# A two-layer attention and expert kernel on one core: the second layer's probabilities turned by VectorE and by transfers in place of TensorE

## The reference

```python
x = x + L0_attention(layernorm(x), ctx)      # 16 heads of width 8
x = x + L0_experts(layernorm(x))             # 8 experts, the best 2 of each row
# second layer, attention: 16 heads of width 64
q, (k, v) = layernorm(x) @ Wq, split(ctx @ Wkv)
dots = q @ k.T * 64 ** -0.5
dots = dots - (1.0 - mask)[:, None, :, None] * 1e6   # mask of the query rows
attn = softmax(dots, axis=-1)
x = x + (attn @ v, heads side by side) @ Wout + bout
x = x + relu(layernorm(x) @ w1 + b1) @ w2 + b2       # width 512
```

## Time and profile before

| | |
|---|---|
| time, three runs | 920.72, 922.16, 922.33 us; median 922.16 |
| the profiled execution: span | 938.3 us (no time of its own is given beside it; it is 16.1 us, 1.75%, above the median) |
| TensorE busy | 875.5 us, 93% |
| ScalarE busy | 691.2 us, 74% |
| VectorE busy | 648.8 us, 69% |
| GpSimd busy | 451.7 us, 48% |
| moved by DMA | 104.82 MB, mean 112 GB/s |

### The profile page before, as it was taken

One profiled execution on the slowest core, in us unless ns is written; L12 is line 12 of the kernel. 1 busy time (PEld: TensorE's weight loads), 2 busy tenths in 40 slices (PEclk: granted clock), 3 DMA queues, 4 the chain that ended last, 5 costly groups with the idle time before them and its releaser, 6 DMA issues.

```text
span 938.3 us, 28898 instructions
## 1 busy us (share of the span) xinstructions
PE 875.5 (93%) x8397; PEld 783.1 (83%) x8397; DVE 648.8 (69%) x2020; ACT 691.2 (74%) x2694; POOL 451.7 (48%) x765
## 2 busy tenths in 40 slices
PE   5889999999999859999997899999999999999996
PEld 3667777777767759999997799999999999999995
DVE  6787888888787652222224888887778777777873
ACT  3988898989889822333336999998877887887782
POOL 3134454544435361111115777776666666666542
PEclk9999999999999988999999999999999999999998
DMA  6896676766767412222231122222211221222110
GB/s 167 247 235 215 199 225 205 217 217 214 238 216 227 121 62 68 68 67 67 73 101 29 40 65 63 62 68 66 65 60 43 67 61 41 65 64 62 36 52 9
DMA packets 114371, 104.82 MB, mean 112 GB/s; under 512 B 10932, under 2 KB 101430, under 8 KB 114294
## 3 DMA queue, kind: packets, MB, share of 16 engines
q1 hardware_dynamic: 107394, 89.64, 31.9%
q0 software_dynamic: 6112, 13.90, 4.8%
q10 hardware_dynamic: 788, 0.39, 0.1%
HBM read 57.32 MB, written 46.58 MB: 111 GB/s over the span
## 4 chain that ended last, share of the span: by engine, by line
PE 82%; issue 5%; DVE 4%; ACT 3%; DMA 2%; SPq 2%; POOL 2%; another core or an unknown queue 0%; POOLq 0%; DVEq 0%
PE bank L1388 10%; PE bank L1155 8%; PE bank L1201 8%; PE bank L1403 7%; PE bank L1360 7%; PE bank L1367 7%; PE bank L1413 6%; PE bank L1474 6%; PE bank L1462 4%; PE bank L1193 4%; PE bank L1485 3%; PE bank L1312 3%; PE bank L1272 2%; PE bank L1177 2%; ACT PR L680 2%
## 5 line engine op out<-in xcount | busy, mean ns | idle before, releaser
L680 ACT ACTIVATE PR<-PR,nmx 128x128 f32<-128x128 f32 x512 | 198.1, 391 | 3.8 <-DVE nmx L881 0.4
L680 ACT ACTIVATE PR<-bank,nmx 128x128 f32<-128x128 f32 x512 | 187.0, 427 | 1.1 <-DVE nmx L881 1.1
L345 POOL TENSOR_TENSOR PR<-PR,rden 128x512 f32<-128x512 f32 x128 | 133.4, 1042 | 98.5 <-DVE rden L886 92.3
L1155 PE MATMUL bank<-ident,PR 128*128 128x128 f32 x1024 | 154.9, 276 | 3.1 <-POOL PR L345 1.0
L1155 PEld LDWEIGHTS bank<-ident,PR 128*128 128x128 f32 x1024 | 120.0, 142 | 43.9 <-issue 38.8
L680 ACT ACTIVATION_READ_ACCUMULATOR PR<-bank,nmx 128x1 f32 x512 | 137.1, 268 | 0.0
L774 ACT ACTIVATE H<-bank 128x512 f32<-128x512 f32 x70 | 41.8, 597 | 91.9 <-PE bank L1360 91.9
L1388 PE MATMUL bank<-XCT,wqk 128*128 128x128 f32 x832 | 103.6, 278 | 0.7 <-ACT XCT L668 0.7
L1388 PEld LDWEIGHTS bank<-XCT,wqk 128*128 128x128 f32 x832 | 96.9, 192 | 3.5 <-ACT XCT L668 1.0
L680 ACT ACTIVATION_READ_ACCUMULATOR PR<-PR,nmx 128x1 f32 x512 | 97.1, 190 | 0.0
L881 DVE TENSOR_REDUCE nmx<-bank 128x4 f32<-128x512 f32 x128 | 86.0, 673 | 7.3 <-PE bank L1193 7.1
(11 more groups left out here) (182 smaller groups left out, 2017.9 us busy)
## 6 DMA issues: line engine op xcount, KB each, us to landing
second_layer_values<-wide SPq DMA_DIRECT2D x32, 512.0 KB
wide<-second_layer_values SPq DMA_DIRECT2D x32, 512.0 KB
expert_outputs<-HF SPq DMA_DIRECT2D x32, 256.0 KB
expert_outputs<-HF SPq DMA_DIRECT2D x64, 128.0 KB
KBD<-expert_outputs SPq DMA_DIRECT2D x64, 128.0 KB
QS<-expert_outputs SPq DMA_DIRECT2D x32, 256.0 KB
PR<-expert_inputs SPq DMA_DIRECT2D x36, 128.0 KB, 2.0
expert_outputs<-PR POOLq DMA_DIRECT2D x35, 128.0 KB, 2.0
```

The costliest lines, as they stand in the source:

```text
L345: nc.gpsimd.tensor_tensor(unit, unit, rden[:, p, G * g:G * g + G].unsqueeze(2).broadcast_to([P, G, P]), ALU.mult).then_inc(s["nm"], 1)
L680: last = nc.scalar.activation(PR[:, g, j * P:(j + 1) * P], scored, ACT.Exp, bias=nmx[:, p, h:h + 1], accum_out=den[:, p, h:h + 1])
L1155: last = nc.tensor.transpose(T_BANK[g % 2][:, j * P:(j + 1) * P], PR[:, g, j * P:(j + 1) * P], ident[:])
```

## The change

The second layer no longer turns the probabilities on TensorE. Instead VectorE turns each unit in blocks of 32 by 32 from `PR` to a new buffer `BT` (`turn_unit`), one instruction a unit, and the blocks are put in their places through DRAM: SP stores half of a sequence (two units, 512 KB) from `BT` to `turned_blocks` (`store_blocks`) and loads it back to `PTC` in four transfers of 128 KB, one for each 32 partitions, in runs of 1 KB (`load_turned`). `transpose_unit` and `read_PT` stay for the first layer alone. Banks 2 and 3 are free by this, and the four units of scores lie in four banks (`S1_BANK`), so that both pairs are multiplied one after the other. ScalarE, not VectorE, copies Y's group 3 (semaphore `yq`). `values` reads `PTC` in runs of 32 elements. TensorE projects group 1 before group 0. All five engines get new orders in `step1`: on ScalarE four `fill_rows` and then all 16 exponentials; on VectorE four row maxima, then the rest; on GpSimd the scaling of unit 2 a step earlier. A few semaphores are merged, with the same meaning. Nothing of what is computed changes.

The core of the diff (the merged semaphores, the lines that adapt the counts in waits, and allocations are left out):

```diff
-        PTC = w1[:, 0:NU, :]
+        PTC = w1[:, 0:NU, :].rearrange("p (a u) c -> p a (u c)", a=2).rearrange("p a (i h b) -> p a i h b", i=4, b=32)
...
+        BT = sb("BT", [P, 2, 2 * G * P])
...
+            def store_blocks(m, half):
+                wait_apart(sp, (c["bt"], NU * m + 2 * half + 2), (c[f"pt{half}"], 64 * m))
+                sp.dma_start(bt_dram[half], BT[:, half, :]).then_inc(c[f"bw{half}"], 16)
+            def load_turned(m, half):
+                wait_apart(sp, (c[f"bw{half}"], 16 * (m + 1)), (c["pv"], NU * (m - 1) + 2 * half + 2))
+                for j in range(4):
+                    sp.dma_start(PTC[32 * j:32 * j + 32, half, :, :, :].rearrange("a i h b -> a i (h b)"),
+                                 bt_dram[half].rearrange("(i a) (j c) -> j a i c", a=32, j=4)[j]).then_inc(c[f"pt{half}"], 16)
             def step1(n, p):
                 q = 1 - p
+                if exists(n - 1):
+                    load_turned(n - 1, 0)
+                    store_blocks(n - 1, 1)
                 if exists(n + 2) and not early(n + 2):
                     load_ctx(sp, c, n + 2, p)
                 if exists(n):
                     wait(sp, c["pv"], NU * (n - 1))
                     sp.dma_start(V1[:, p, :, :].rearrange("p h d -> p (h d)"), v_dram[n]).then_inc(c[f"v{p}"], 16)
+                if exists(n - 1):
+                    load_turned(n - 1, 1)
                 if exists(n - 3):
                     wait(sp, d["x"], n - 2)
                     sp.dma_start(out[n - 3], acc[:, q, :]).then_inc(out_stored[q], 16)
+                if exists(n):
+                    store_blocks(n, 0)
             over_steps(sp, step1, -3, NB + 2, 3, KEYS_AHEAD)
             sp.wait_ge(out_stored[0], 8 * NB)
             sp.wait_ge(out_stored[1], 8 * NB)
@@ -625,7 +646,7 @@
             def step1(n, p):
                 q = 1 - p
                 if exists(n - 1):
...
-                if exists(n - 1):
-                    scale_pool(pool, c, n - 1, q, 3)
-                if exists(n - 2):
-                    norm_pool(pool, d, n - 2, p)
                 if exists(n + 2):
                     norm_pool(pool, c, n + 2, p)
-                if exists(n):
-                    scale_pool(pool, c, n, p, 0)
-                    scale_pool(pool, c, n, p, 1)
                 if exists(n + 1):
                     wait_apart(pool, (c["xn"], n + 2))
                     xrow = X[:, bass.ds(n + 1, 1), :].rearrange("p o d -> p (o d)")
                     nc.gpsimd.tensor_tensor(xrow, xrow, out_bias[:, 0, :], ALU.add).then_inc(c["bias"], 1)
+                if exists(n):
+                    scale_pool(pool, c, n, p, 0)
+                if exists(n - 2):
+                    norm_pool(pool, d, n - 2, p)
+                if exists(n):
+                    scale_pool(pool, c, n, p, 1)
+                    scale_pool(pool, c, n, p, 2)
             over_steps(pool, step1, -3, NB + 2, 3, KEYS_AHEAD)
 
 
...
-                    exponentials(c, n, p, 1)
-                    fill_rows(n, 2)
-                if exists(n - 1):
-                    read_PT(c, n - 1, 3)
-                if exists(n):
-                    fill_rows(n, 3)
-                    exponentials(c, n, p, 2)
-                if exists(n - 1):
-                    read_heads(n - 1, q, 0)
-                if exists(n + 2):
-                    read_xct(c, n + 2, p, not early(n + 2), c["y"], NU * (n + 1))
-                if exists(n - 1):
-                    read_heads(n - 1, q, 1)
-                if exists(n):
-                    exponentials(c, n, p, 3)
+                    act.wait_ge(c["y"], NU * n + NU)
+                    wait(act, c["s"], NU * (n - 1))
+                    nc.scalar.activation(YT[:, p, 3 * G:4 * G, :].rearrange("p h s -> p (h s)"), Y_BANK[3][:],
+                                         ACT.Copy).then_inc(c["yq"], 1)
                 if exists(n + 1):
-                    fill_rows(n + 1, 0)
-                    fill_rows(n + 1, 1)
-                if exists(n):
-                    read_PT(c, n, 1)
-                if exists(n + 1):
-                    exponentials(c, n + 1, q, 0)
+                    read_xct(c, n + 1, q, not early(n + 1), c["y"], NU * n)
+                if exists(n - 2):
+                    read_heads(n - 2, p, 0)
+                    read_heads(n - 2, p, 1)
+                if exists(n):
+                    for g in range(NU):
+                        fill_rows(n, g)
+                    for g in range(NU):
+                        exponentials(c, n, p, g)
             over_steps(act, step1, -3, NB + 2, 3, KEYS_AHEAD)
 
 
...
+                def turn_unit(m, g):
+                    dve.wait_ge(c["nm"], NU * m + g + 1)
+                    wait(dve, c[f"bw{g // 2}"], 16 * m)
+                    nc.vector.transpose(BT[:, g // 2, :].rearrange("p (j h b) -> p h j b", j=4, b=32)[:, G * (g % 2):G * (g % 2) + G],
+                                        PR[:, g, :].rearrange("p (h j b) -> p h j b", h=G, j=4)).then_inc(c["bt"], 1)
 
...
                     keys = key_slot(m) if early(m) else KT1[:, p, :, :]
-                    if isinstance(m, int) and m == 0:
-                        pe.wait_ge(kg["kc"], 2 * KEYS_AHEAD)
-                    wait(pe, c["yc"], NU * m + NU)
-                    wait(pe, c["sh"], NU * m + 2 * pair)
+                    wait(pe, c["sh"], NU * (m - 1) + 2 * pair + 2)
                     for j in range(G):
                         chunk = G * pair + j
                         for r in range(2):
                             half = slice(DH1 * r, DH1 * r + DH1)
-                            last = mm(S_BANK[r][:, j * P:(j + 1) * P], QT1[half, p, chunk, :], keys[half, chunk, :],
+                            last = mm(S1_BANK[2 * pair + r][:, j * P:(j + 1) * P], QT1[half, p, chunk, :], keys[half, chunk, :],
                                       start=True, stop=True)
                             if j == G - 1:
                                 last.then_inc(c["s"], 1)
@@ -1410,22 +1423,20 @@
                     for j in range(G):
                         for r in range(2):
                             half = slice(DH1 * r, DH1 * r + DH1)
-                            last = mm(bank[5 + pair][half, j * P:(j + 1) * P], V1[:, p, 2 * (G * pair + j) + r, :],
-                                      PTC[:, 2 * pair + r, j * P:(j + 1) * P], start=True, stop=True)
+                            last = mm(bank[5 + pair][half, j * P:(j + 1) * P].rearrange("p (i b) -> p i b", i=4),
+                                      V1[:, p, 2 * (G * pair + j) + r, :], PTC[:, pair, :, G * r + j, :], start=True, stop=True)
                             if j == G - 1:
...
+                    if is_sequence(0, n):
+                        pe.wait_ge(kg["kc"], 2 * KEYS_AHEAD)
+                    wait(pe, c["yc"], upto(n, 3, 2))
+                    wait(pe, c["yq"], upto(n))
                     scores(n, p, 0)
+                    scores(n, p, 1)
                 if exists(n - 3):
                     wait(pe, d["xct"], n - 2)
```

134 lines of the change are left out of this document (59 added, 75 removed).

## The result

| | before | after | ratio, 95% interval |
|---|---|---|---|
| time, median of four runs each | 921.44 us | 937.09 us | 1.0186 [1.0162, 1.0211] |
| lowest and highest | 919.52, 922.33 | 935.17, 940.22 | |

The account below looks back on a forecast made before the run. TensorE bounds the kernel before; after the change a loop over three engines was to bind. Start +3.5, early +5.5, late -10 and end +3.4 gave +2.4 on the span, 922.2 + 2.3 = 924.5 us; range 907 to 942.

Parts of the forecast that it names:

- the likeliest case: Three-engine loop in the second layer, with the norm meeting GpSimd's scaling: 924.5 us, own range 917.5 to 931.5, chance 0.38.
- TensorE's clock: Rival: TensorE idles 2.5 us in early steps and its clock falls in a third of them: +11, 935 us; chance 0.11.
- Early steps: Steps with keys made ahead: 12.4 us between first scores, 0.7 longer each, +5.5 us over eight.
- The loop: Second-layer steps run from scores through ScalarE, VectorE and GpSimd back to TensorE: 13.2 us late, 12.4 early.
- Step 4: VectorE turns unit 0 from 7.2 to 7.8; its norm waits for GpSimd's scaling until 8.9; two norms end at 9.4.
- Step 6: Early: reciprocal, turn of unit 1, copy to `XDT` that bank 7 waits for, 10.4; inputs and values: next scores at 12.4.
- The turn: VectorE's block turn of one unit, taken at 0.60 us, like the maximum of 512 columns; four a step.
- The second rival: A VectorE turn takes twice, 1.2 us, and VectorE becomes the bound: 949 us; chance 0.15.
- The first three intervals: Start of the second layer, between first scores: from 10 us growing to 12.4, 33.5 in all, +3.5.
- The way through DRAM: Store 2.9 and load 3.4 us, covered by 3 us: nothing in steps. Rival, late transfers: 940 us, chance 0.11.
- Values in runs of 32 elements: TensorE's values read in runs of 32: taken at nothing, at worst twice the 1.73 us.
- TensorE alone binds: Rival: TensorE's own work sets the second layer, all else hidden: 877 us; chance 0.05.

Follow-up runs that it names:

- e6: Changed kernel with plain transfers in place of the second layer's gathers (routing of the experts' results left out): 954.0 us, ratio 1.013 to the kernel before.
- e8: Changed kernel without gathers, plus idle TensorE products in the first 11 steps: 944.4 us, ratio 1.005 to the kernel before.
- e5: Changed kernel with VectorE's late-step norm directly behind the turn of unit 0, ahead of the copies of Y: 985.8 us, ratio 1.049 to the kernel before.
- e3: Changed kernel without the way through DRAM and without VectorE's turns: 952.9 us, ratio 1.015 to the kernel before.
- e0: Changed kernel itself, unedited, measured again on a chip where the kernel before takes 941.0 us: 976.7 us, ratio 1.040.
- e2: Changed kernel without the way through DRAM (stores, loads and their waits removed): 965.0 us, ratio 1.025 to the kernel before.
- e7: Kernel before with plain transfers in place of the second layer's gathers: 940.9 us, ratio 1.001 to the unedited kernel before.
- e1: Changed kernel with idle TensorE products at the end of steps 0 to 10: 967.7 us, ratio 1.028 to the kernel before.

## Why the prediction was right and wrong

The direction was right, and 937.1 lies in the range of 907 to 942. It lies outside the 917.5 to 931.5 that the likeliest case gave itself: what brings it in is the room left for the rivals. The sum was 13.3 us short, and the rival that came true had been given 0.11: TensorE's clock, with 935 us. That this figure is within 2 us is luck in part. The rival let the clock fall in a third of the early steps at up to 3 us; it fell in all of them, at 1.5 where nothing else disturbs, and the other terms missed by several us each, up and down (the sum again, below).

Of its signs these came: late steps between 12.5 and 14, waits ahead of line 1404 for the copy of Y, line 330 at 1 us early, a turn of 0.70 us (0.63 start to start), a DMA share of 0.71 at 217 GB/s. Early steps of 12.4 did not come, nor did the wait for `XDT`. And TensorE's waits name DMA, 1.9 us in two late steps, which by its own words counts against it.

- **TensorE's clock.** The forecast took its work at full clock. It fell in each early step, for 3.4 us (6.8 in the first two falls), behind a wait of 2 us or more, much as the rival put it (idle 2.5 us). The rival priced it at 11; fill products bring back 8.9 (e6 against e8), and in the steps it is 13.57 against 12.05 where nothing else disturbs. This is the largest missing term. A share of busy time near 93% says nothing of it; the forecast loop did, since it put the idle time in one piece.
- **The loop.** Right in its course, and somewhat too long. Step 4 let the norm end its wait with the scaling and then do its own work. In fact it ends with the scaling, at 573.84 + 1.06 = 574.90 against 573.77 + 1.04 = 574.81 on GpSimd. And late the copy of group 1, which the step left out, stands between turn and norm. So VectorE has copied group 0 by 787.50 - 777.92 = 9.6 us, not 10.2, and a late step is 12.9, not 13.2: -13.5 over twenty, not -10, with the two waits for turned blocks in it (-15.6 in e6). The run with the norm right behind the turn (e5) shows what the forecast's own order would have cost.
- **Early steps.** Step 6 took the copy to `XDT` for what bank 7 waits for. The chain shows the norm's own turn on TensorE, line 1524, and behind it group 3. At full clock that is 12.05, not 12.4. The eight came to +14.6 instead of +5.5, since the clock adds 1.5 to each.
- **The turn** was taken at 0.60 from start to start and is 0.63: right. It does not wait for GpSimd's scaling, as the norm does: its maximum over 128 is 0.714, while 66 of the 128 run beside a scaling for over 0.2 us, and on the chip of e0 a turn from 807.98 to 808.65 lies over a scaling from 808.13 on at its usual 0.67. The second rival (twice as long) is out.
- **The first three intervals**: +9.3 instead of +3.5. The first was foreseen (10 us; 10.3). The next two are 14.5 each, where at most 12.4 was allowed. The clock is at half for 6.8 us from 493.6 and again from 507.3, and fill brings 1.1 to 1.4, though half clock does not go away altogether. Leaving out turns and transfers brings 4.0 (e3 against e0, on two chips). What remains, some 4, was not taken apart; it may lie in the order.
- **The way through DRAM.** "Costed at nothing" held for the steps as they came out: without it (e2) all 31 together are 1.7 us shorter. It holds only because they are long (e8). At the end the term was too small, +3.4 for 6.9. SP's timeline, then TensorE's:

```profile
906.94 1.76 SPq L540 DMA_DIRECT2D w<-turned_blocks  x4
908.79 0.38 SPq L534 DMA_DIRECT2D turned_blocks<-BT  x1
912.33 1.74 SPq L540 DMA_DIRECT2D w<-turned_blocks  x4
```

```profile
914.32 1.09 PE L1426 MATMUL bank<-w,wide 128*64 128x128 f32 x16
916.80 1.93 PE L1426 MATMUL bank<-w,wide 128*64 128x128 f32 x16 [1.39 <-DMA w<-turned_blocks]
```

The last turn ends at 906.2, but its store is queued behind the load of the first half and is issued at 908.8. The second pair's values come 916.8 - 894.3 = 22.5 us after the last first scores; 20.5 were forecast, 17.1 is the old value. From the last turn to these values the forecast had 20.5 - 12.2 = 8.3 us, and 6.3 of them were the store and its load. The trace has 10.6: 2.6 in SP's queue, where the forecast saw "nothing else to be late with", and 8.0 for store and load. So the transfers were dearer, by 1.7 here, and on the page too: 4.0 us for the store (2.9 assumed) and 3.1 for a load (2.0 assumed). What is left of the 6.9, about 1.5, lies behind: the second pair's values take 1.93 us, at half clock from 916.9 on, and what follows them about 0.8 more than before.
- **Values in runs of 32 elements** were costed at nothing: sixteen products take 1.09 us at full clock (914.32), half of the old thirty-two's 1.97. Right.
- **TensorE alone binds**, 877 us, is out, as the forecast said: it needs the loop to be wrong in two places.

**The sum again**, with what was measured against the kernel before, in the kernel pair without gathers and with fill (e8 against e7): start +8.1, early +7.3, late -16.4, rest +8.3, together +7.4; and the clock 8.9, together 16.3. The measured differences are 17.2 in the traces and 15.6 in the medians. Against the forecast's +3.5, +5.5, -10 and +3.4 the start was too small by 4.6 and the end by 4.9, and the late steps were better by 6.4: three misses that partly cancel, beside the clock.

## What to carry to other kernels

When a full engine is relieved, ask where its idle time will lie. Here it did not spread: it collected in front of one wait of the new loop, 2 us in each early step, and behind it the clock fell, so the work that was left got dearer. Cost the first and last steps of a pipeline apart from its steady ones: here the steady late steps kept what was promised, and start, early steps and end gave it back twice over. And what a full engine hides (a late signal, a transfer) can become visible when it is full no more, so measure a change on more than one chip before believing 1%.

## What the runs showed of the hardware

- **Signals are late around indirect transfers, on some chips.** On chips where the kernel before takes 940 us and not 921, a signal of TensorE came 1.1 us late by ScalarE's waits in each late step while GpSimd issued its gathers (e0; e1 has 16.7 us over 16 on another chip). With plain transfers in place of these this is gone, and 18.4 us with it (465.2 to 446.8, on two chips); moving them by 1.8 us took 14.9 (to 450.3). In the kernel before neither shows: ScalarE's waits are the same with gathers and without. That the gathers cause it is shown; how, and why the chips differ, is open.
- **The first layer may be the same.** It scatters rows by 64 indirect transfers. VectorE's waits there, 60 to 300 us, on one of these chips and then in the profile after:

```profile
DVE OT L995 <- PE bank L1217: 27.1, 21, 1.5
```

```profile
DVE OT L995 <- PE bank L1217: 4.1, 13, 0.6
```

The profile of the kernel before has 26.3 us over 21 for this wait. That would explain the 21 us between the two profiles ahead of the second layer. It was not tried.
- **A norm of 128 columns that starts beside a scaling of GpSimd ends only with it; the block turn does not wait.** The norm takes 1.054 against 0.33 us alone, and 128 turns take 0.667 to 0.714, 66 of them beside a scaling. The Trainium skill (SBUF — State Buffer, Who interferes with whom) states that copies and operations with one scalar can take the ports that VectorE shares with GpSimd, and that the later one of the two then waits; the trace agrees for the norm. For the turn it is this case's runs that show it. By the Trainium skill (VectorE: DVE Perf Modes, The three transpose paths) four turns of 128 x 128 would be 1.24 us, an estimate from a figure in bf16; a unit of four took 0.70 in float32. So the price of the turn did not speak against this change; what spoke against it was the loop.
